# Perceiver on one core: the context phase with keys made transposed, key stores of one 128-row tile each, and all maxima of a block among the key tiles of the next

## What is computed

```python
xn = layer_norm(ctx, gamma_x, beta_x); ln = layer_norm(layer_norm(x), gamma_l, beta_l)
q = (ln @ Wq) * 64 ** -0.5
k = concat(rope(xn @ Wkv[:, :512]), ln @ Wkv[:, :512])       # 8 heads of 64
v = concat(xn @ Wkv[:, 512:], ln @ Wkv[:, 512:])
x = x + softmax(q @ k.T) @ v @ Wo                            # then layers and experts
```

## Time and profile before

| | |
|---|---|
| median of 3 runs | 2415.43 us (2414.27 to 2417.82) |
| profiled execution, time / span | 2416.9 / 2415.0 us |
| TensorE matmuls busy | 2234.4 us, 93% |
| VectorE, ScalarE, GpSimd busy | 73%, 47%, 41% |
| granted TensorE clock, mean | 0.97 of full speed |
| DMA queue of SP | 242.44 MB, 31.3% of 16 engines' time |

### The profile page before, as it was taken

The page is one execution under the profiler, slowest core; times in us unless marked ns, Lnnn a source line. Parts: engine busy times, 40 slices in busy tenths (PEclk is TensorE's granted clock), DMA queues, the critical chain, the costliest instruction groups (busy, mean ns, idle before and its releaser), DMA issues. The chain is left out here.

```text
span 2415.0 us, 40033 instructions
## 1 busy us (share of the span) xinstructions
PE 2234.4 (93%) x13127; PEld 1132.7 (47%) x13239; DVE 1764.6 (73%) x2652; ACT 1134.1 (47%) x1722; POOL 990.5 (41%) x651
## 2 busy tenths in 40 slices
PE   6899999998989989989889999999999999999858
PEld 2344444442323223223247575756657575756433
DVE  6788888877979989978856666757565666667573
ACT  4232333223444444545456564646465565646353
POOL 0233343336979979968522222213031222222040
PEclk9999999998999999989899999999999999999978
DMA  3233333325322333333133324233333233242230
GB/s 122 77 110 109 109 111 125 110 74 164 90 78 85 85 120 89 85 113 87 45 114 123 114 88 147 72 106 96 122 96 124 97 123 114 88 137 82 87 107 20
DMA packets 156204, 244.05 MB, mean 101 GB/s; under 512 B 12096, under 2 KB 64448, under 8 KB 156096
## 3 DMA queue, kind: packets, MB, share of 16 engines
q1 hardware_dynamic: 156096, 242.44, 31.3%
HBM read 205.71 MB, written 36.70 MB: 100 GB/s over the span
## 5 line engine op out<-in xcount | busy, mean ns | idle before, releaser
L820 POOL TENSOR_TENSOR h_lo<-h_lo,probs 128x896 f32<-128x896 f32 (+1 forms) x272 | 546.8, 2010 | 48.6 <-ACT probs L931 28.1
L59 PE MATMUL l_mm<-l_xt_hi,wt_hi 128*128 128x256 f16 (+3 forms) x1568 | 420.2, 279 | 2.3 <-DVE l_xt_lo L1261 1.5
L61 PE MATMUL l_mm<-l_xt_hi,wt_lo 128*128 128x256 f16 (+3 forms) x1568 | 419.5, 278 | 0.4
L60 PE MATMUL l_mm<-l_xt_lo,wt_hi 128*128 128x256 bf16 (+3 forms) x1560 | 417.1, 278 | 0.0
L1220 POOL TENSOR_TENSOR l_rstd<-l_var_eps,neg_half 128x1 f32<-128x1 f32 x68 | 65.6, 965 | 847.1 <-DVE l_var_eps L1272 847.1
L931 ACT ACTIVATE probs<-sc 128x1024 f32<-128x1024 f32 x272 | 274.4, 1023 | 285.2 <-PE sc L979 232.3
L876 DVE TENSOR_TENSOR h_lo<-h_lo,probs 128x128 f32<-128x128 f32 (+1 forms) x272 | 290.6, 1068 | 22.9 <-ACT probs L931 22.2
L835 DVE TENSOR_REDUCE pmax<-mx 128x1024 f32 x204 | 248.9, 1220 | 36.8 <-PE mx L966 28.4
L990 PE MATMUL pv<-probs,vb 128*64 128x512 f32 x1088 | 267.1, 612 | 0.0
L978 PE MATMUL sc<-q_hi,ka 128*128 128x512 f16 x544 | 212.4, 390 | 8.4 <-ACT q_lo L914 5.2
L61 PE MATMUL l_tok<-wt_hi,h_lo 128*128 128x512 f16 x576 | 218.3, 379 | 1.7
(11 more groups left out here) (272 smaller groups left out, 3926.6 us busy)
## 6 DMA issues: line engine op xcount, KB each, us to landing
stage<-in_L_attn_Wf SPq DMA_DIRECT2D x64, 1024.0 KB, 5.4
keys<-wt_hi SPq DMA_DIRECT2D x34, 512.0 KB, 3.9
ka<-keys SPq DMA_DIRECT2D x136, 128.0 KB, 2.7
vb<-values SPq DMA_DIRECT2D x68, 256.0 KB, 2.8
stage<-in_ctx SPq DMA_DIRECT2D x16, 1024.0 KB, 5.2
values<-wt_lo SPq DMA_DIRECT2D x16, 1024.0 KB, 6.2
stage<-in_L_ffn_f SPq DMA_DIRECT2D x16, 1024.0 KB, 5.3
kh<-keys SPq DMA_DIRECT2D x68, 128.0 KB, 2.7
```

The costliest lines, as they stand in the source:

```text
L59: pe.matmul(out, lh, rh, start=first, stop=False, **kw)
L60: pe.matmul(out, lh, rl, start=False, stop=False, **kw)
L61: return pe.matmul(out, ll, rh, start=False, stop=last, **kw)
L820: g.tensor_tensor(sums[:, mine], sums[:, mine], probs[j][:, mine], ALU.add)\
```

## The change

Keys are projected with the weights as the fixed operand and 512 rows as the moving one, so that a tile of 128 features by 512 rows comes out transposed. The columns of Wkv are reordered on the host (key_order): tile 2g holds the first halves of heads 4g to 4g+3, tile 2g+1 the second halves. Key transposes and their copies go. VectorE makes two products for each tile, with the bias as a scalar for each partition (bias_cols); GpSimd adds or subtracts the tiles; ScalarE and GpSimd write hi and lo straight into the store buffers. The value bias is taken out of the context: the latents' values are stored less the bias (VectorE), and the attention's output gets it (out_high, out_low). ScalarE copies the values of the context. The table of cos and sin lies by features now, 512 KB a block. Heads 0 and 1 of the hi keys are copied from SBUF to SBUF into km[u], four transfers of 32 rows, and keys are stored in eight transfers of 128 KB. The maxima of block b-1 are four pairs, one behind each of the four key tiles of block b, with a buffer of 1024 columns; the values and transposes follow. Projections have four PSUM buffers (pj), keys and then values of the same number. Normalisation of block b+1 is VectorE's first work in block b, statistics of block b+2 come late in it. In the latents, bias comes before the values, and is transposed.

Core of the diff (unchanged and removed lines are largely left out; a line of ... stands for them):

```diff
-    sp.dma_start(k.k_store(0, CTX_BLOCKS), kt_hi).then_inc(stored, 16)
+    for rows, tile in KM_ROWS:
+        sp.dma_start(k.km[1][rows, :], kt_hi[tile[0], tile[1], :]).then_inc(km_in, 16)
+    for g in range(PAIRS):
+        sp.dma_start(k.k_store(0, CTX_BLOCKS, g), kt_hi[:, g, :]).then_inc(stored, 16)
     sp.wait_ge(lo_copied, 2 * PAIRS + PAIRS)
-    sp.dma_start(k.k_store(1, CTX_BLOCKS), kt_lo).then_inc(stored, 16)
+    for g in range(PAIRS):
+        sp.dma_start(k.k_store(1, CTX_BLOCKS, g), kt_lo[:, g, :]).then_inc(stored, 16)
     sp.wait_ge(v_copied, TT)
     sp.dma_start(k.v_store(CTX_BLOCKS), v_out[:]).then_inc(stored, 16)
-    sp.wait_ge(stored, 48)
+    sp.wait_ge(km_in, 16 * len(KM_ROWS))
+    sp.wait_ge(stored, 16 * (2 * PAIRS + 1))
...
+    dve.wait_ge(bias_copied, 2)
+    for t in range(TT):
+        dve.wait_ge(mm_ready, 2 * PAIRS + 2 + t + 1)
+        v.tensor_tensor(v_out[:, :, t, :], mm[(t + 2) % 4][:].rearrange("p (a d) -> p a d", a=PAIRS),
+                        k.kv_bias[:, D:2 * D].rearrange("p (a d) -> p a d", a=PAIRS),
+                        ALU.subtract).then_inc(v_copied, 1)
+    dve.wait_ge(turned, 1)
+    for n in range(2):
+        v.tensor_copy(k.bias_cols[:, n * CH:(n + 1) * CH],
+                      tp[n][:].rearrange("p (c n) -> p c n", n=P)[:, :, 0]).then_inc(cols_copied, 1)
...
     pe.wait_ge(beta_done, CH)
     for n in range(2):
-        pe.wait_ge(v_copied, n + 1)
+        pe.wait_ge(lo_copied, 2 * PAIRS + n + 1)
         for c in range(CH):
             m = t_.matmul(mm[n][:], beta_cols[:, c, :], wkv[:, c, n * D:(n + 1) * D],
                           start=c == 0, stop=c == CH - 1)
         m.then_inc(mm_ready, 1)
+    for t in range(TT):
+        if t < 2:
+            pe.wait_ge(lo_copied, 2 * PAIRS + t + 3)
+        else:
+            pe.wait_ge(bias_copied, t - 1)
+        for c in range(CH):
+            rows = slice(t * P, (t + 1) * P)
+            m = product3(t_, mm[(t + 2) % 4][:], (lat_hi[:, c, rows], lat_lo[:, c, rows]),
+                         (wkv_hi[:, c, D:], wkv_lo[:, c, D:]), c == 0, c == CH - 1)
+        m.then_inc(mm_ready, 1)
+    for n in range(2):
+        for c in range(CH):
+            m = t_.transpose(tp[n][:, c * P:(c + 1) * P], k.kv_bias[:, (n * CH + c) * P:(n * CH + c + 1) * P],
+                             k.ident[:])
+    m.then_inc(turned, 1)
 k.spare_semaphores = sems
...
+    def store_keys(i, u, hl, tile):
+        sp.dma_start(k.k_store(hl, 2 * i + u, tile), kt[u][:, hl, tile, :]).then_inc(stored[u], 16)
+    load_tab(0, 0)
+    load_raw(1, 0)
+    load_tab(0, 1)
     def body(i, u):
         b = 2 * i + u
...
+        sp.wait_ge(k_hi_done, 4 * b + 2)
+        sp.sem_inc(passed, 1)
+        if not is_zero(b):
+            sp.wait_ge(mx_ready, TT * b)
+            sp.sem_inc(passed, 1)
+        for rows_, (part, g) in KM_ROWS:
+            sp.dma_start(km[u][rows_, :], kt[u][part, 0, g, :]).then_inc(km_in[u], 16)
+        for hl, done in enumerate((k_hi_done, k_lo_done)):
+            if hl:
+                sp.wait_ge(done, 4 * b + 2)
+                sp.sem_inc(passed, 1)
+            for tile in range(2):
+                store_keys(i, u, hl, tile)
+        for hl, done in enumerate((k_hi_done, k_lo_done)):
+            sp.wait_ge(done, 4 * b + 4)
+            sp.sem_inc(passed, 1)
+            for tile in range(2, 4):
+                store_keys(i, u, hl, tile)
+        if before_end(i, u, 2):
+            sp.wait_ge(k_mult, 8 * b + 8)
+            sp.sem_inc(passed, 1)
+            load_tab(*after(i, u, 2))
+        if before_end(i, u, 3):
             sp.wait_ge(norm_done, SUB * b + SUB)
             sp.sem_inc(passed, 1)
...
+            load_raw(*after(i, u, 3))
         sp.wait_ge(v_copied, SUB * b + SUB)
         sp.sem_inc(passed, 1)
         sp.dma_start(k.v_store(b), vo[u]).then_inc(stored[u], 16)
...
+        def turn(n):
+            pool.wait_ge(k_mult, 8 * b + 4 * n + 3)
+            g.tensor_tensor(a_cos[n], a_cos[n], b_sin[n], ALU.subtract).then_inc(k_added, 1)
+            pool.wait_ge(k_mult, 8 * b + 4 * n + 4)
+            g.tensor_tensor(b_cos[n], b_cos[n], a_sin[n], ALU.add).then_inc(k_added, 1)
+        def key_low(n):
+            for m, turned in enumerate((a_cos[n], b_cos[n])):
+                tile = 2 * n + m
+                pool.wait_ge(k_hi_done, 4 * b + tile + 1)
+                if not is_first(i) and tile == 0:
+                    pool.wait_ge(stored[u], STORES * i)
+                g.tensor_tensor(kt[u][:, 1, tile, :], turned, kt[u][:, 0, tile, :],
+                                ALU.subtract).then_inc(k_lo_done, 1)
+        for n in range(2):
+            turn(n)
+            key_low(n)
+        if before_end(i, u, 2):
+            rstd_of(b + 2)
...
+    def products(i, u, tile):
+        b, n = 2 * i + u, tile // 2
+        dve.wait_ge(k_ready, 4 * b + tile + 1)
+        if tile == 0:
+            dve.wait_ge(tab_in[u], 16 * (i + 1))
+        if not is_zero(b):
+            dve.wait_ge(k_hi_done, 4 * (b - 1) + 2 * n + 2)
+            dve.wait_ge(k_lo_done, 4 * (b - 1) + 2 * n + 2)
+        first, second = ((a_cos[n], 0), (a_sin[n], 1)) if tile % 2 == 0 else ((b_sin[n], 1), (b_cos[n], 0))
+        for out, trig in (first, second):
+            v.scalar_tensor_tensor(out=out, in0=pj[tile][:], scalar=k.bias_cols[:, tile:tile + 1],
+                                   in1=tab[u][:, trig, :], op0=ALU.add, op1=ALU.mult).then_inc(k_mult, 1)
+    def unit_max(index, j, column):
+        dve.wait_ge(mx_ready, index + 1)
+        v.tensor_reduce(maxima[:, :, column(j)], mx[:], AX_X, ALU.max).then_inc(mx_done, 1)
+    def latent_column(j):
+        return slice(j * KB + CTX_BLOCKS, j * KB + CTX_BLOCKS + 1)
     for c in range(CH):
         low(0, 0, c)
+    norm_stats(0, 1)
     def body(i, u):
...
         b = 2 * i + u
...
+        if before_end(i, u, 1):
+            normalise(*after(i, u, 1))
+        def earlier_max(j):
+            if is_zero(b):
+                unit_max(j, j, latent_column)
+            else:
+                unit_max(TT * b + j, j, lambda j: bass.ds(j * KB + b - 1, 1))
+        for tile in range(TT):
+            products(i, u, tile)
+            earlier_max(tile)
+        if before_end(i, u, 1):
+            low(*after(i, u, 1), 0)
+            low(*after(i, u, 1), 1)
+        if before_end(i, u, 2):
+            norm_stats(*after(i, u, 2))
+        if before_end(i, u, 1):
+            low(*after(i, u, 1), 2)
+        if before_end(i, u, 1):
+            low(*after(i, u, 1), 3)
     over_blocks(dve, body)
...
+    def key_high(i, u, tile):
+        act.wait_ge(k_added, 4 * (2 * i + u) + tile + 1)
+        if not is_first(i) and tile == 0:
+            act.wait_ge(stored[u], STORES * i)
+            act.wait_ge(km_in[u], 16 * len(KM_ROWS) * i)
+        a.activation(kt[u][:, 0, tile, :], (a_cos, b_cos)[tile % 2][tile // 2], ACT.Copy).then_inc(k_hi_done, 1)
+    def values(i, u, t):
+        act.wait_ge(v_ready, SUB * (2 * i + u) + t + 1)
         if not is_first(i) and t == 0:
...
+            act.wait_ge(stored[u], STORES * i)
+        a.activation(vo[u][:, :, t, :], pj[t][:].rearrange("p (a d) -> p a d", a=PAIRS),
+                     ACT.Copy).then_inc(v_copied, 1)
...
+        more = before_end(i, u, 1)
+        nxt = after(i, u, 1)
         key_high(i, u, 0)
         key_high(i, u, 1)
...
+        values(i, u, 0)
         key_high(i, u, 2)
...
         if more:
             high(*nxt, 0)
             high(*nxt, 1)
         key_high(i, u, 3)
+        values(i, u, 1)
         if more:
             high(*nxt, 2)
+        values(i, u, 2)
+        if more:
             high(*nxt, 3)
...
+        values(i, u, 3)
...
+    def keys(i, u, tile):
         b = 2 * i + u
...
         pe.wait_ge(xt_lo_done, CH * b + CH)
...
+        if not is_zero(b):
+            pe.wait_ge(v_copied, SUB * (b - 1) + tile + 1)
+        cols = slice(tile * P, (tile + 1) * P)
         for c in range(CH):
...
+            m = product3(t_, pj[tile][:], (k.wg_hi[:, c, cols], k.wg_lo[:, c, cols]),
+                         (xt_hi[u][:, c, :], xt_lo[u][:, c, :]), c == 0, c == CH - 1)
+        m.then_inc(k_ready, 1)
     def values(i, u, t):
...
+        pe.wait_ge(k_mult, 8 * (2 * i + u) + 2 * t + 2)
+        rows_ = slice(t * P, (t + 1) * P)
+        for c in range(CH):
+            m = product3(t_, pj[t][:], (xt_hi[u][:, c, rows_], xt_lo[u][:, c, rows_]),
+                         (k.wg_hi[:, c, D:], k.wg_lo[:, c, D:]), c == 0, c == CH - 1)
+        m.then_inc(v_ready, 1)
+    def unit_max(index, slot, j, loads):
+        if loads is not None:
+            pe.wait_ge(km_in[slot], 16 * len(KM_ROWS) * loads)
+        if not (isinstance(index, int) and index == 0):
+            pe.wait_ge(mx_done, index)
+        for s in range(2):
+            part = slice(s * HD, (s + 1) * HD)
+            m = t_.matmul(mx[:, s, :], k.q_hi[part, s, j * P:(j + 1) * P], km[slot][part, :],
```

(102 more changed lines are left out.)

307 lines of the change are left out of this document (67 added, 240 removed).

## The result

The changed kernel takes 2342.31 us, median of 4 (2339.8 to 2343.26), beside 2414.85 (2414.08 to 2417.82) for the kernel before on the same chip: ratio 0.9696, 95% interval 0.9679 to 0.9713. The forecast was 2339, range 2332 to 2358, faster with 0.94.

What follows compares the result with a forecast made beforehand. TensorE and VectorE were both taken as nearly full in the context blocks. Terms +4.65, -4.4, -67.5, -9.65 and 0 sum to -76.9 us, from 2416.9 to 2340, stated as 2339; range 2332 to 2358, chance 0.81.

Steps and rivals of the forecast that it cites:

- 24.23: Context blocks: predicted TensorE work in us per full block, against 29.05 before; over blocks 1 to 14, -67.5 us.
- C: Rival on TensorE's maxima: the two matmuls of a pair do not overlap, 0.86 us more a block; 2352 us, chance 0.05.
- The stall of 1.35: TensorE's wait on VectorE per context block, 1.35 us, predicted to vanish if VectorE keeps up.
- -1.80: TensorE per context block: keys come out transposed, so the key transposes go, saving 1.80 us.
- -1.67: TensorE per context block: eight maxima become four pairs, each costing 0.42 us like a single, saving 1.67 us.
- B: Rival on VectorE: its products are held by GpSimd; 2370 to 2390 us, say 2380, chance 0.07.
- A: Rival on VectorE: it still sets the maxima and 1.35 us a block of waiting stays; 2359 us, chance 0.12.
- SP's queue: SP in a context block: 15 transfers for 5, 0.4 to 0.5 us of issue each, 7 of 24.2 us.
- D: Rival, slower than before: the hi-key copy for the maxima lands late in SP's queue; 2432 us at 23 us landing, chance 0.04.
- Latents: Before the context: the value store is no longer hidden and SP waits for its landing, +4.65 us, bounds +4.2 and +6.
- tail: Block 15 and the end of the context: four pairs of maxima replace eight singles, 39.75 to 30.1 us, -9.65.
- The attention: Attention after the context: same bytes and unchanged loop instructions, so 0 us, bounds -1 and +1.

Runs made afterwards that it cites:

- the kernel with both edits: The kernel before with only four of the eight maxima per block and without the key transposes and their copies; 2367.14 us.

## Why the prediction was right

Forecast -76.9, measured -73.6 between the profiled spans.

- **The pace.** "24.23" against 24.18. TensorE's work was read rightly from spacings of starts: 2.59 for a projection, 0.42 for a pair, checked by the run without pairs at 0.43. C (pairs don't overlap) falls with it.
- **"The stall of 1.35 goes if VectorE keeps up."** It did, and the condition carries more than the sentence says. The three terms -1.80, -1.67 and -1.35 add up in this change but are not three savings: in the kernel before, the first two alone bring 3.0 instead of 3.5 plus a stall gone, and 1.75 needs VectorE's new order and the new banks. In the order in which the runs took them away, VectorE's order, the banks and ScalarE's value copies together are worth more (1.75) than the key transposes (0.4 to 0.85), and the prediction gave them no price of their own. No run has the new order with the old maxima and transposes, so what it would bring there is not shown.
- **VectorE.** Taken 0.75 for a product, measured median 0.744 and never above 0.753 in 128, with GpSimd busy in 43% of blocks 7 to 14 (83.33 of 193.50): B is dead. The row agrees with the rule of the Trainium skill, SBUF — State Buffer, "Who interferes with whom", if a scalar column is not counted as a second input. Cover 0.31 instead of 0.17. A (some stall stays) fell in blocks 1 to 14, and the runs with an added operation show that it was 0.3 us a tile away.
- **SP's queue.** "0.4 to 0.5 us of issue each, 7 of 24.2" was low: eight key stores took 7.88, 1.0 each, and the four copies 2.5, so with table, rows and values about 12. No wait came of it, because cover was 16.8; D never had its condition.
- **Latents** +4.24 for +4.65, **block 0** -4.46 for -4.4, **tail** -9.9 for -9.65.
- **The step that failed:** "The attention: one load for two of the keys, same bytes, and no instruction of its loop changes; scale and bias folded into two operations a pair: 0, bounds -1 and +1." It cost +4.5, outside its bounds. I compared bytes and instructions and not the access pattern: the load for the maxima kept its 128 KB but became 2 x 64 rows, and it is first in the queue. The other terms came out 1.7 us better in sum (+4.24 - 4.46 - 68.49 - 9.91 = -78.6), so the total was 3.3 off and inside the range. The total is nearer than its worst term in part because these errors have opposite signs.

## What to carry to other kernels

Work taken off the bounding engine is worth its time only as far as the engine it waits for is in order: find what stands ahead of the operation that frees a single buffer, and move bursts (statistics, normalisation) to where no buffer waits. When a layout changes, check the access pattern of every transfer that reads it, above all those that are wanted at once behind a barrier, and not the bytes. A term that adds up in the sum should not be told as a saving by itself until it has been taken alone.

## What was not expected of the hardware

Issue times on SP differ: in block 7 the key stores of 128 KB took 1.0 us each, the load of rows and the value store 0.4, the table 0.7. What was issued before counts too: the same load of keys took 1.72 right behind the two loads for the maxima (475.15) and 0.40 in the run that issues those behind it.

Two kernels with a changed context lost time where their code is the same as before. In the one without maxima TensorE pauses in the layers' projections with nothing to wait for, 23.6 us after 1050 us (0.2 in the kernel before), nearly all of it in six pauses of 3.2 to 4.2 us, about 138 us apart. In the one without transposes it is 12.6 us, in six pauses of about 2. One pause of each:

```profile
1308.08 0.48 PE L61 MATMUL l_mm<-l_xt_hi,wt_lo 128*128 128x384 f16 x1 [4.16 <-issue]
```

```profile
1348.75 0.32 PE L60 MATMUL l_mm<-l_xt_lo,wt_hi 128*128 128x384 bf16 x1 [2.00 <-issue]
```

That is why the first saves 56.1 us up to the first scores (485.16 to 429.05 from the first key matmul) and only 22 in all: from the first scores to the end it takes 1890.5 and not 1855.6. The pauses are 23.4 of these 34.9. Most of the rest is the clock: in the 8 us behind each of the six pauses the granted clock is 0.79 to 0.83, which by (1 - clock) x 8, as an estimate, is 10 us together.

No other run has above 3.4 us of such pauses. The cause stays open. A shorter program ahead of these loops is not enough for it: the kernel with both edits has fewer instructions than the one without transposes (38392 against 38807) and pauses for 0.6 us.
